# First batch's projection in another order, stacked scratch for q and k, and the last output tiles one by one: a transformer layer on one Trainium2 core

## The reference, cut to what matters

```python
x = L0_attn_x                                    # (4, 1024, 256): 4 batches, 1024 tokens
q = heads(binlinear(layernorm(x), Wq, bq))       # 16 heads of 16; likewise k and v
att = softmax(einsum('bhtd,bhsd->bhts', q, k) * 16 ** -0.5)
y = einsum('bhts,bhsd->bhtd', att, v)
x = x + layernorm(binlinear(merge(y), Wp, bp))
h = silu(layernorm(x) @ w1.T * s1) * (layernorm(x) @ w2.T * s2)   # 256 -> 1024
h = gelu(h @ h1.T * sh1); h = gelu(h @ h2.T * sh2)                # 1024 -> 1024, twice
x = x + layernorm(h @ w3.T * s3)                                  # 1024 -> 256
# binlinear(x, W, b) = x @ (sign(W) * mean(abs(W), rows)).T + b
```

## Time and profile before

| what | value |
|---|---|
| median of 3 runs | 1284.57 us |
| profiled execution, its time | 1285.64 us |
| its span, first to last instruction | 1283.9 us |
| PE busy | 1193.3 us, 93% |
| ACT busy | 726.2 us, 57% |
| DVE busy | 631.1 us, 49% |
| POOL busy | 78.6 us, 6% |
| granted TensorE clock, mean | 0.983 |

### The profile page before, as it was taken

The page is one execution under the profiler, slowest core; times in us unless marked ns, Lnnn a source line. Parts: engine busy times, 40 slices in busy tenths (PEclk is TensorE's granted clock), DMA queues, the critical chain, the costliest instruction groups (busy, mean ns, idle before and its releaser), DMA issues.

```text
span 1283.9 us, 17482 instructions
## 1 busy us (share of the span) xinstructions
PE 1193.3 (93%) x6705; PEld 727.1 (57%) x6705; DVE 631.1 (49%) x1150; ACT 726.2 (57%) x866; POOL 78.6 (6%) x78
## 2 busy tenths in 40 slices
PE   3299989999999999998999999999999999999997
PEld 3123222323232322224888888888888888888886
DVE  6234433444353431442656747646577376575523
ACT  4288979898989899997324224233242342432411
POOL 5101110111011100000000000000000000000000
PEclk9689999999999999999999999999999999999999
DMA  3868567776765678512010201001001010010000
GB/s 114 225 175 229 132 158 160 181 183 165 153 173 158 195 162 156 89 33 66 1 34 1 66 1 34 33 1 41 26 14 53 1 34 33 1 33 1 17 1 17
DMA packets 52712, 107.55 MB, mean 84 GB/s; under 512 B 6544, under 2 KB 23312, under 8 KB 52620
## 3 DMA queue, kind: packets, MB, share of 16 engines
q1 hardware_dynamic: 52332, 105.54, 32.5%
q10 hardware_dynamic: 288, 0.79, 0.5%
HBM read 71.94 MB, written 45.88 MB: 92 GB/s over the span
## 4 chain that ended last, share of the span: by engine, by line
PE 53%; DVE 0%; issue 0%; ACT 0%; POOLq 0%; DVEq 0%
PE ffn_ps L1601 23%; PE ffn_ps L1600 23%; PE ffn_ps L1628 2%; PE ffn_ps L1629 2%; PE side_ps L1584 1%; PE side_ps L1593 0%; DVE ln_stats L1731 0%; DVE zn L1742 0%; DVE zn L1783 0%; DVE zn L1793 0%; DVE ln_mean_var L1735 0%; ACT ln_std L1669 0%; DVE ln_rstd L1739 0%; POOLq L1538 0%; DVEq L1781 0%
## 5 line engine op out<-in xcount | busy, mean ns | idle before, releaser
L1210 ACT ACTIVATE probs<-s_ps 128x1024 f32<-128x1024 f32 x512 | 477.0, 1054 | 71.9 <-PE s_ps L1054 71.6
L1601 PE MATMUL ffn_ps<-h_lo,W 128*128 128x512 f32 x1024 | 405.9, 396 | 0.0
L1600 PE MATMUL ffn_ps<-h_hi,W 128*128 128x512 f32 x1024 | 403.0, 394 | 0.0
L1066 PE MATMUL y_ps<-probs,v_st 128*17 128x512 f32 x2048 | 272.0, 603 | 34.1 <-ACT probs L1210 17.2
L1601 PEld LDWEIGHTS ffn_ps<-h_lo,W 128*128 128x128 f32 x1024 | 192.0, 188 | 47.5
L1600 PEld LDWEIGHTS ffn_ps<-h_hi,W 128*128 128x128 f32 x1024 | 191.9, 187 | 45.7
L1690 ACT ACTIVATE hid<-ffn_ps,scales 128x512 f32<-128x512 f32 x128 | 80.9, 685 | 240.0 <-PE ffn_ps L1601 235.0
L1054 PE MATMUL s_ps<-q_st,k_st 50*128 50x512 f32 x1024 | 190.0, 449 | 20.3 <-DMA q_st<-shift 19.6
L1054 PEld LDWEIGHTS s_ps<-q_st,k_st 50*128 50x128 f32 x1024 | 77.5, 187 | 200.4 <-ACT probs L1210 163.1
L1807 DVE CAST h_hi<-hid 128x512 fp32r<-128x512 f32 x128 | 53.4, 417 | 192.8 <-ACT hid L1690 192.7
L1801 DVE TENSOR_TENSOR h_lo<-hid,h_hi 128x512 fp32r<-128x512 f32 x192 | 130.0, 684 | 1.1
(11 more groups left out here) (156 smaller groups left out, 944.8 us busy)
## 6 DMA issues: line engine op xcount, KB each, us to landing
q_st<-q_scr SPq DMA_DIRECT2D x96, 128.0 KB, 7.4
k_st<-k_scr SPq DMA_DIRECT2D x90, 128.0 KB, 4.6
w_scr<-ffn_w SPq DMA_DIRECT2D x16, 704.0 KB, 7.8
W<-w_scr SPq DMA_DIRECT2D x16, 704.0 KB, 6.2
y_scr<-y_sb SPq DMA_DIRECT2D x32, 256.0 KB, 2.2
v_st<-v_scr SPq DMA_DIRECT2D x16, 272.0 KB, 8.7
y<-y_scr SPq DMA_DIRECT2D x16, 256.0 KB
sums<-y_scr SPq DMA_DIRECT2D x16, 256.0 KB
```

Source lines behind the costliest of these rows:

```text
L1066: i = pe.matmul(y_ps[32 * j:32 * j + VCOLS, :], v_st[g % 2][:, s, VCOLS * j:VCOLS * (j + 1)], probs[turn % 2][j // 2][:, j % 2, :], start= ...
L1210: act.activation(probs[turn % 2][pp][:, :, :], s_ps[a % 3][:, :, :], ACT.Exp, scale=SCALE).then_inc(probs_ready, 1)
L1600: pe.matmul(bank_of(t)[:, :], w, hi[:, k, :].bitcast(form), start=(k == 0), stop=False)
L1601: mm = pe.matmul(bank_of(t)[:, :], w, lo[:, k, :].bitcast(form), start=False, stop=last)
```

## The change

1. Scratch: q_scr and k_scr become (64 heads, 48 rows, 1024), the finished stacks. Each part is stored once for each place where it stands: three stores a tile in place of two. A quad is loaded by four DMAs of 48 rows (`load_stacks`) in place of twelve of 16.
2. The first batch: POOL fills the rows of k_st0 first, waits until block 0 is normalised, then fills those of q_st1. DVE fills q_st0's before x lands, ACT writes the ones of k_st1 as the sign of a constant. w_nat is loaded after the two x and the two w_tr.
3. q and k are projected in halves; half 0 holds heads 0 to 7, with quads 0 and 1. Its high part is taken by DVE (block 0) or ACT (block 1); squares go to POOL, but for the last. Half 0's eight stores come first (`hi_stored`, `lo_stored`), then the first quad's loads in an order that differs between SP and ACT, then v, and last the other 16 stores, whose semaphore `stored` SP awaits before it loads quad 1.
4. Last block of the tail: tiles 0 to 3 one by one on four banks (`last_tiles`), and norm, residual and store for each tile (`last_out`, `last_store`).

```diff
 def load_stacks(sp, q_scr, k_scr, q, k, g, done):
-    load_k(sp, k_scr, k, g, done)
-    load_q(sp, q_scr, q, g, done)
+    for hh in range(2):
+        for st, scr in ((k, k_scr), (q, q_scr)):
+            sp.dma_start(rows_of(st, hh, 0, PARTS), heads_of(scr, g, hh, 0, PARTS)).then_inc(done, 16)
...
+def chunk_rows(scr, b, c, i, u):
+    heads = P // HEAD_DIM
+    first = b * HEADS + c * heads
+    return scr[first:first + heads, i * HEAD_DIM:(i + 1) * HEAD_DIM, u * BLK:(u + 1) * BLK]
...
+            sp.wait_ge(high_by_dve, 1)
+            store(HI, 0, 0, hi_stored, once)
+            sp.wait_ge(low_done, 1)
+            store(LO, 0, 0, lo_stored, every)
+            sp.wait_ge(high_by_act, 1)
+            store(HI, 1, 0, hi_stored, once)
+            sp.wait_ge(low_done, 2)
+            store(LO, 1, 0, lo_stored, every)
...
+            sp.wait_ge(hi_stored, 16 * 2 * BATCH_BLOCKS)
+            for i, hh in ((0, 0), (1, 1), (0, 1), (1, 0)):
+                sp.dma_start(rows_of(quads.q[0], hh, i, 1), heads_of(q_scr, 0, hh, ROWS_OF_Q[HI][0], 1))\
+                    .then_inc(quads.loaded[0], 16)
...
+            sp.wait_ge(v_stored, 16 * (BATCH_BLOCKS + 1))
+            load_v(sp, v_scr, quads, 0, 0)
+            sp.dma_start(m_scr[0, 0:HEADS], shift[:, :].bitcast(F32)).then_inc(shift_stored, 16)
+            sp.wait_ge(high_by_act, 3)
+            for u in range(BATCH_BLOCKS):
+                store(HI, u, 0, stored, again)
+                store(HI, u, 1, stored, every)
+            for u in range(BATCH_BLOCKS):
+                sp.wait_ge(low_done, 3 + u)
+                store(LO, u, 1, stored, every)
...
+            for hh in range(2):
+                fill(quads.k[0], hh, 1.0, hh)
+            pool.wait_ge(norm_done, TILES)
+            for hh in range(2):
+                fill(quads.q[1], hh, 0.0, 2 + hh)
...
+            for i, hh in ((0, 1), (2, 0), (0, 0), (2, 1)):
+                act.dma_start(rows_of(quads.k[0], hh, i, 1), heads_of(k_scr, 0, hh, ROWS_OF_K[HI][0], 1))\
+                    .then_inc(quads.loaded[0], 16)
...
                     load_xb(0)
+                    sp.wait_ge(stored, 16 * REST_STORES)
                     load_quad(sp, q_scr, k_scr, v_scr, quads, 1, 1)
...
+                early, late = range(HT - 2), range(HT - 2, HT)
...
+                for a in range(2):
+                    tile_part(a, early)
+                for a in range(2):
+                    tile_part(a, late).then_inc(tile_done, 1)
+                for a in range(2, TILES):
+                    tile_part(a, range(HT)).then_inc(tile_done, 1)
...
+                head(0)
+                for a in range(1, TILES):
+                    head(a)
+                    rest(a - 1)
+                rest(TILES - 1)
```

More of the change, by code:

```diff
@@ L230, in layer @@
             shift_stored=keep.enter_context(nc.semaphore("shift_stored")),
-            stored=[keep.enter_context(nc.semaphore(f"stored{u}")) for u in range(2)],
+            stored=keep.enter_context(nc.semaphore("stored")),
         )
@@ L351, in project, with column @@
         shift_done = sem("shift_done")
+        hi_stored = sem("hi_stored")
+        lo_stored = sem("lo_stored")
+        v_stored = sem("v_stored")
         stored = quads.stored
+        ALL_SET, ROWS_SET, SMALL = 5, 4, 16 * 5
         block = ctx.enter_context(nc.Block())
[L360 to L369, removed]
+        def column(s):
+            return (s % 2) * CT + s // 2
         def v_shaped(row):
@@ L374, in v_shaped, with constant_rows @@
                 .to_broadcast([P, HEADS // QUAD, TILES, QUAD, HEAD_DIM])
-        def is_first(n):
-            return isinstance(n, int) and n == 0
+        def constant_rows(st, hh):
+            return st[hh * HALF + ONES_FROM:hh * HALF + STACK_M, :, :].rearrange("p j t -> p (j t)")
         @block.sync
         def _(sp):
[L381 to L400, removed]
-                sp.dma_start(v_rows[0, :, :, TILES * u:TILES * (u + 1), :].rearrange("q p s n -> p q (s n)"),
-                             v_aug[u][:, :, :, :, :].rearrange("p q t j n -> p q (t j n)")).then_inc(stored[u], 16)
-            load(0, 0)
-            sp.dma_start(w_tr[:, 0:2, :, :], attn_wT[:, 0:2]).then_inc(tr_loaded, 16)
@@ new lines, in store, with store_v @@
+            def store(s, u, c, done, copies):
+                for z, (scr, rows) in enumerate(((q_scr, ROWS_OF_Q), (k_scr, ROWS_OF_K))):
+                    for i in rows[s][copies]:
+                        sp.dma_start(chunk_rows(scr, 0, c, i, u), part[s][u][:, 2 * c + z, :].bitcast(F32))\
+                            .then_inc(done, 16)
+            once, again, every = slice(0, 1), slice(1, None), slice(0, None)
+            def store_v(u):
+                sp.wait_ge(aug_done, u + 1)
+                sp.dma_start(v_rows[0, :, :, TILES * u:TILES * (u + 1), :].rearrange("q p s n -> p q (s n)"),
+                             v_aug[u][:, :, :, :, :].rearrange("p q t j n -> p q (t j n)")).then_inc(v_stored, 16)
@@ L501, in _, with top_norm @@
-            steps(first, body)
-            dve.wait_ge(norms_read, BATCH_BLOCKS + 1)
+            def top_norm(u):
+                dve.wait_ge(norms_done, u + 1)
+                dve.tensor_reduce(const.top_norms[:, u:u + 1], norm_ps[u], AX.X, ALU.max).then_inc(norms_read, 1)
+            dve.memset(eps[:, :], EPS).then_inc(eps_set, 1)
+            for hh in range(2):
+                dve.memset(constant_rows(quads.q[0], hh).bitcast(F32), 0.0).then_inc(rows_set, 1)
+            statistics(0)
@@ L605, in body, with high_of_x @@
[L605 to L619 removed]
+            def high_of_x(u):
+                act.wait_ge(xT_done, u + 1)
+                act.activation(x_hi[u][:, :, :], xT_ps[:, :, :], ACT.Copy).then_inc(x_hi_done, 1)
```

524 lines of the change are left out of this document (274 added, 250 removed).

## The result

The changed kernel is slower: 1296.19 us median of 6 runs (1291.37 to 1298.93), against 1284.64 of the kernel before (1283.95 to 1289.58, 6 runs), ratio 1.0081 with a 95% interval of 1.0065 to 1.0098. That is slower by 0.8%, clear of the noise. The forecast was 1275.6, range 1265 to 1282. One execution of the kernel before took 1766.45 us, at a granted clock of 0.614, and is left out of the ratios of merged_first, rest_first and memset_later.

A forecast was written before the change was run, and what follows sets the result against it. The prediction took ACT and PE as the limit in attention, PE in the tail, and waiting chains in the start. Gains of 5.2 (start) and 3.7 (end) took 1285.64 to 1276.7, less 1.07 for the median: 1275.6, range 1265 to 1282.

The forecast's parts named there:

- Step 1: Start: with only two POOL memsets ahead, DVE's four scalings take 1.38 us instead of 7.64; 6.3 us gained, x ready at 9.0.
- Step 2: First projection in halves: ACT begins block 1's high part at 24.9 us; last of four critical parts done at 29.1.
- Step 3: First-batch transfers: 8x16x512 stores use half the engines, 1.37 us each; first quad's loads run at 220 GB/s.
- R: Point in the start when v's load and the shift's store have been issued, forecast at 46.1 us.
- Rival 1: Start: stores use all engines, 0.69 us each, first scores at 51.6, total 1268.2 us; chance 0.17.
- Step 4: End of the start: SP issues 16 stores at 0.65 us each, 10.4 us; first scores at 58.6.
- step 5: Early attention: x's load, behind 22 us of store backlog, lands at 71.4, 0.5 us late; quad 1's loads hidden.
- Attention, taken at 0: Attention and steady tail: changed loads and stores lie beside PE and ACT, so no time gained or lost.
- Rival 4: Attention: DVE waits for stored parts before reusing slots, PE loses 18 us, total 1293.6 us; chance 0.06.
- The end: Behind the last matmul: finishing and storing the last tiles one by one gains 3.7 us.
- Rival 2: Start: first quad's loads stay at 129 GB/s, 12.2 us, and DVE memsets cost more; total 1281 to 1283; chance 0.16.
- Rival 3: Last tiles: PE loses what DVE gains, so 3.7 us less gained, total 1279.3 us; chance 0.07.

The follow-up runs named there:

- merged_first: Changed kernel with only the first projection's 24 q and k stores written as 128 rows in one run, attention's left as 8x16 rows: 1283.46 us, ratio 0.9980.
- rest_first: old_layout with its 8 rest stores issued ahead of SP's wait for the stores of v: 1268.37 us, ratio 0.9863.
- memset_later: Kernel before the change with POOL's 8 memsets of constant rows put behind the second block's x_norm: 1282.31 us, ratio 0.9974.
- merged_rows: Changed kernel with every q and k part store written as 128 rows in one run instead of 8 heads x 16 rows: 1276.01 us, ratio 0.9930.
- rest_first_heads: Changed kernel with its 16 rest stores issued ahead of SP's wait for the stores of v: 1295.99 us, ratio 1.0092.
- shift_first: Changed kernel with v's wait and load put behind the store of the shift at each batch switch: 1287.02 us, ratio 1.0018.
- tail_only: Kernel before the change with only the last block's tiles finished and stored one by one: 1281.79 us, ratio 0.9983.
- old_layout: Changed kernel's first-batch order and last tiles on the old scratch (128-row stores, 8 rest stores, 12 loads a quad): 1271.48 us, ratio 0.9900.

## Why the prediction was wrong, point by point

- *Step 1, memsets*: right. x ready at 9.2 (forecast 9.0); the memsets on DVE took 1.76 each, ended at 5.42 and held the statistics back from 5.14 to 5.46 at most.
- *Step 2, halves*: right in kind, 2.8 us too careful. Last critical part at 26.3 (forecast 29.1). POOL's squares beside DVE made 2.80 and 1.93 of a subtraction, which is the 2 us supposed; but ACT began the high part at 23.24 instead of 24.9, and the longer of the two was not on block 1's path.
- *Step 3, form and R*: the form is right, share 0.52 and 1.28 us a store against 1.37. R at 45.7 against 46.1 is right in part by luck. The forecast let all loads begin at 34.4 and had v stored 10.8 us later. SP began them at 31.48, since the high parts have a semaphore of their own, and v's stores had landed at 44.8, 13.3 us later. From 34 to 39 us, with loads of q and k and a store of v in the queues, 179 GB/s moved in all, less than the 220 taken for the loads alone. The Trainium skill's rule on the slowest dimension (DMA: Bandwidth & Descriptors, section Why a DMA increments its semaphore by 16 and not by 1) held: eight heads, half the engines, and merged_rows, which gives the same bytes 128 rows, share 1.03. Rival 1 did not come.
- *Step 4, 16 stores ahead of the barrier*: this is the step that failed. It priced an issue at 0.65 us as if SP could run ahead of its transfers without end, while step 5 counted 22 us of backlog for the very same stores. The first two (four in rest_first_heads) cost 0.65, the others what they take to move: 18.6 us instead of 10.4. The barrier then took 3.1 us to SP's next issue (64.34 to 67.43) where 1.9 was taken, for which no run shows a reason, and the first score is at 67.6 instead of 58.6. merged_rows shows the term by itself: where a store moves in 0.68 us, 10.6 us and 57.2. The trace of before had a row that said so, which the prediction did not use. Four stores of 512 KB (1.37 us at 382 GB/s) went out at the end of its projection, and the last took 1.38 us to issue where its like took 0.47:

```profile
41.61 0.37 SPq L398 DMA_DIRECT2D q_scr<-part  x1
42.02 1.38 SPq L398 DMA_DIRECT2D k_scr<-part  x1
```

- *Step 5, what is late next*: wrong with step 4, and harmless. As SP was held, there was hardly a backlog when x's load went out. It landed 4.8 us after the first score:

```profile
72.44 1.41 DVE L1247 BATCH_NORM_STATS2 pj_stats<-zn 128x6 f32<-128x256 f32 x4 [6.70 <-DMA zn<-x]
```

- *Attention, taken at 0*: the second step that failed, by 6.1 us in the profiled execution and 8.7 in the second; more than 2 us was the prediction's own sign of being wrong. The argument was that no wait of PE or ACT on a DMA was large; it did not ask how near one was. The shift row of a new quad was one, at 0.2 us of wait already in the kernel before. SP's list is in order: slow part stores made v's store late, SP stood for v, and the shift and the weights behind it were late; PE's clock fell after the waits. Rival 4 had the sign and nearly the time (1293.6), but not the place: DVE has no wait for stored parts among its largest, and shift_first removes the loss without touching a part's slot.
- *The end*: right in kind, 3.1 instead of 3.7, since DVE's 1.97 us a tile leaves it behind PE. That 3.6 was measured against a forecast of 3.7 is luck: the other 0.5 is the clock at the entry to the ffn. From the first to the second table load it takes 15.0 us in both profiles of the kernel after, 15.5 before and 16.1 to 16.7 in the others. The granted clock around the first table load stands at 0.50 for 6.8 us in tail_only and memset_later, for 3.4 us in the kernel before and the rest, and not at all in the two profiles of the kernel after. Why it did not fall there was not tried.
- *Rival 2* (loads no faster): its late R (5.1 to 7.1 us) did not come. The 129 GB/s itself is not refuted: what moved from 32 to 44 us, 223 to 273 GB/s, holds the stores of v, and the loads of q and k alone, 1.57 MB from 31.48 to about 43, took some 12 us, as this rival has it. What saved R is that they began early and that the stores of v ran beside them, not behind. No run tries the order of the loads by itself. *Rival 3* (the end gives nothing): out, by the 3.1 us.

With step 4 at its measured 18.6 the forecast's own sum would have had the first score at 46.1 + 18.6 + 2.1 = 66.8, 2.5 us later than before, and with the end's 3.7 a gain of 1.2, less than the 2.6 that the prediction held to be measurable. Attention's loss made it slower.

## What to carry to other kernels

The stores whose outer dimension is 8 ran at half the speed here (share 0.52 against 1.03), and SP got only a few of them ahead: price a long row of DMAs ahead of a barrier by the time they take to move, not to issue, and keep the layout in which stores run over all engines even if loads then need three times as many DMAs (old_layout: 1271.5 against 1296.2). Where one engine issues everything in order, ask of each slower store what stands behind the next wait on its list; moving one 64 KB store ahead of such a wait was worth 8.5 us, and with it the slow form cost attention nothing (535.2 against 536.6 before).

## What the hardware showed unexpectedly

- SP issued two to four stores of 8x16x512 (256 KB) at 0.65 us each, then it was held at 1.2 us each; in the form of 128 rows the held pace was 0.64 to 0.67, and 8 went out in 5.4 us behind loads still on their way.
- Waits of PE of 1.7 to 4.1 us in attention went with a granted clock of 0.50 for 3.4 or 6.8 us, the longer stretch also after the shortest wait, and 5.6 us of waits came with 10.1 us more of attention than without them.
- POOL's squares of 128x1024 beside DVE's subtraction of the same size made it 2.80 and 1.93 us, where half of the 2.27 in the earlier trace rows is 1.14.
